# Normalised x of batches 2 to 7 is transposed by 32 x 32 turns on VectorE and sixteen transfers per batch, instead of on TensorE

## The reference, cut to what matters

```python
xn = layernorm(x)                        # per row of 128
q, k = rope(xn @ Wq.T), rope(xn @ Wk.T)  # 16 heads of 8; rope's angle is the batch's
v = xn @ Wv.T
attn = softmax(q @ k.T / sqrt(8)) @ v    # per batch and head, 512 x 512
# experts: sigmoid router (32 experts in 8 groups of 4, best 4 groups, best 6 experts)
moe = sum_e combine[:, e] * relu(xn @ up[e].T) ** 2 @ down[e].T      # 32 experts, 64 wide
shared = relu(xn @ shared_up.T) ** 2 @ shared_down.T                 # 256 wide
out = x + attn + moe + shared
```

## Time and profile before

| what | us |
|---|---|
| three runs, median (lowest to highest) | 612.33 (611.86 to 616.31) |
| the profiled execution, its own time | 611.43 |
| its span, first to last instruction | 609.6 |
| TensorE busy in it | 603.1 |
| VectorE, ScalarE, GpSimd busy in it | 425.5, 407.9, 428.4 |

### The profile page before, as it was taken

One profiled execution on the slowest core, in us unless ns is written; L12 is line 12 of the kernel. 1 busy time (PEld: TensorE's weight loads), 2 busy tenths in 40 slices (PEclk: granted clock), 3 DMA queues, 4 the chain that ended last, 5 costly groups with the idle time before them and its releaser, 6 DMA issues.

```text
span 609.6 us, 20168 instructions
## 1 busy us (share of the span) xinstructions
PE 603.1 (99%) x8269; PEld 269.1 (44%) x8269; DVE 425.5 (70%) x1058; ACT 407.9 (67%) x803; POOL 428.4 (70%) x512
## 2 busy tenths in 40 slices
PE   9999999999999999999999999999999999999997
PEld 7432544444444444434444434454443444444343
DVE  7898965777767776677867778586766877666402
ACT  3578667766776666766667676676667666666664
POOL 5850478677896778867788678876776767667653
PEclk9999999999999999999999999999999999999999
DMA  5176743646446254652437454263544634343430
GB/s 149 32 218 200 165 115 88 216 105 158 111 94 206 59 151 111 205 145 70 122 80 243 106 154 104 68 209 85 140 112 145 191 80 113 75 106 71 106 72 18
DMA packets 52029, 76.19 MB, mean 125 GB/s; under 512 B 5985, under 2 KB 19169, under 8 KB 51937
## 3 DMA queue, kind: packets, MB, share of 16 engines
q1 hardware_dynamic: 51916, 74.90, 45.6%
q10 hardware_dynamic: 20, 0.00, 0.0%
HBM read 56.14 MB, written 18.35 MB: 122 GB/s over the span
## 4 chain that ended last, share of the span: by engine, by line
PE 95%; DVE 2%; DMA 1%; SPq 1%; ACT 0%; issue 0%; DVEq 0%
PE acc L1060 21%; PE pv L1227 20%; PE st L1060 15%; PE upb L1060 10%; PE st L1197 9%; PE sc L1186 6%; PE upb L1197 4%; PE st L1202 3%; PE upb L1202 2%; PE sc L1119 1%; PE st L1169 1%; DVE nmax L930 1%; SPq L361 1%; DMA stacks<-k_stack 1%; DMA k_stack<-qk_parts 1%; PE upb L1169 1%
## 5 line engine op out<-in xcount | busy, mean ns | idle before, releaser
L930 DVE TENSOR_REDUCE nmax<-sc 128x1 f32<-128x512 f32 x512 | 328.5, 686 | 142.7 <-PE sc L1186 131.7
L700 ACT ACTIVATE probs<-st 128x512 f32<-128x512 f32 x359 | 202.8, 595 | 29.1 <-PE st L1202 19.3
L558 POOL TENSOR_TENSOR gated<-gate_at,relu 128x512 f32<-128x512 f32 x111 | 142.0, 1280 | 98.3 <-ACT relu L705 92.0
L562 POOL TENSOR_TENSOR g<-gated,relu 128x512 f32<-128x512 f32 x111 | 142.2, 1281 | 16.2 <-POOL gated L558 0.4
L1202 PE MATMUL st<-stacks 32*128 32x512 f32 x359 | 148.6, 577 | 0.0
L1227 PE MATMUL pv<-probs,v_aug 128*32 128x512 f32 x1024 | 136.4, 605 | 0.1
L1060 PE MATMUL acc<-dn,g 128*32 128x128 f32 x3512 | 134.8, 274 | 0.0
L1186 PE MATMUL sc<-stacks 32*128 32x512 f32 x512 | 132.6, 493 | 0.9 <-DMA stacks<-k_stack 0.4
L1060 PEld LDWEIGHTS acc<-dn,g 128*32 128x32 f32 x3512 | 112.2, 114 | 22.3 <-issue 22.1
L700 ACT ACTIVATE probs<-upb 128x512 f32<-128x512 f32 x153 | 91.0, 595 | 21.0 <-PE st L1202 14.2
L1197 PE MATMUL st<-m_rows,ones 3*128 3x512 bf16 x359 | 99.6, 384 | 0.3 <-ACT sh L682 0.3
(11 more groups left out here) (186 smaller groups left out, 565.4 us busy)
## 6 DMA issues: line engine op xcount, KB each, us to landing
gate_at<-gate_rows SPq DMA_DIRECT2D x62, 512.0 KB, 6.6
stacks<-q_stack SPq DMA_DIRECT2D x30, 256.0 KB, 6.7
stacks<-k_stack SPq DMA_DIRECT2D x30, 256.0 KB, 6.8
q_stack<-qk_parts SPq DMA_DIRECT2D x28, 256.0 KB, 6.6
k_stack<-qk_parts SPq DMA_DIRECT2D x28, 256.0 KB, 5.7
x_res<-in_x SPq DMA_DIRECT2D x8, 256.0 KB, 7.8
out<-y SPq DMA_DIRECT2D x8, 256.0 KB, 7.3
m_rows<-m_parts SPq DMA_DIRECT2D x95, 4.0 KB
```

The source lines that it names most:

```text
L558: nc.gpsimd.tensor_tensor(gated[:, u % 2, :], gate_at[:, group % RING, u % GATES, :], relu[:, u % RELUS, :], ALU.mult).then_inc(gated_read ...
L562: nc.gpsimd.tensor_tensor(g[:, u % 2, :], gated[:, u % 2, :], relu[:, u % RELUS, :], ALU.mult).then_inc(g_ready, 1)
L700: nc.scalar.activation(probs[:, u % 2, h, :], ring_b("st", u * QUAD + h)[:], ACT.Exp).then_inc(probs_ready, 1)
L930: nc.vector.tensor_reduce(out=nmax[:, s % 2, at:at + 1], in_=sc_b[tile % SC_BANKS][:], op=ALU.max, axis=AXX, negate=True).then_inc(s_read, 1)
```

## The change

For batches 2 to 7 the transposes on TensorE, their use of the ring and the copy on ScalarE go. In the same unit VectorE turns the 128 x 512 normalised rows in blocks of 32 x 32 (`turn_x`), into a new tile `x_blk`, laid out so that the piece of 32 columns c of x stands together. After it, SP issues sixteen transfers (`move_x`): for each c and each block a of 32 partitions, the blocks go from partitions 32 a on to partitions 32 c on of `xnT`, 32 partitions x 4 tiles x 32 numbers of 4 bytes, 16 KB. SP does this at the head of step j = 0 of batches 0 to 5, ahead of `load_max` of the next step, and waits there for VectorE. TensorE's projections and `make_half` wait for all sixteen (`x_moved`). GpSimd waits, before it overwrites half of `xn`, for the turn instead of the transposes. VectorE waits, before it overwrites `x_blk`, for the moves of the batch before. A unit that held the transposes no longer counts as `whole`. The first two batches are transposed as before.

```diff
@@ ring_order
                 if b + 2 < B:
-                    if n == (X_UNIT if b else X2_UNIT):
-                        order += [("x", b + 2)]
@@ SP
+            def move_x(i):
+                sp.wait_ge(x_turned, i - 1)
+                rows = xnT[:, i * T:(i + 1) * T].rearrange("d (t a r) -> d t a r", t=TT, r=COL)
+                for c in range(P // COL):
+                    for a in range(P // COL):
+                        sp.dma_start(rows[c * COL:(c + 1) * COL, :, a, :], x_blk[a * COL:(a + 1) * COL, :, c, :]
+                                     ).then_inc(x_moved, 16)
...
             for s in range(STEPS):
                 b, j = s // NQ, s % NQ
+                if j == 0 and b + 2 < B:
+                    move_x(b + 2)
@@ GpSimd, normalise
                 if tiles[0] == 0:
-                    wait(pool, xnT_psum, i - 1)
+                    wait(pool, xnT_psum, min(i - 1, 2))
+                    wait(pool, x_turned, i - 3)
@@ ScalarE, side_out
                 if b + 2 < B:
-                    if n == (X_UNIT if b else X2_UNIT):
-                        turned_out(b + 2)
@@ VectorE
+            def turn_x(i):
+                dve.wait_ge(xn_ready, i)
+                wait(dve, x_moved, (i - 2) * X_MOVES * 16)
+                nc.vector.transpose(x_blk[:].rearrange("p t c r -> p (t c r)"), xn[:, i % 2, :, :].rearrange("p t d -> p (t d)")
+                                    ).then_inc(x_turned, 1)
...
                 if n == SUM_UNIT and b:
                     add_residual(b - 1)
+                if n == (X_UNIT if b else X2_UNIT) and b + 2 < B:
+                    turn_x(b + 2)
@@ TensorE
                 att = kt == ATT_KT and q and q % PAIR == 0
-                return att or (b + 2 < B and n == (X_UNIT if b else X2_UNIT)) or u == UNITS - 1
+                return att or u == UNITS - 1
...
             def project(i, w, at=slice(0, T)):
-                pe.wait_ge(xnT_ready, i + 1)
                 if i > 1:
+                    pe.wait_ge(x_moved, (i - 1) * X_MOVES * 16)
                     bank_free("qk", 2 * i + w)
+                else:
+                    pe.wait_ge(xnT_ready, i + 1)
...
                 made = V_HALVES * (i - 1) + k
+                if i > 1:
+                    pe.wait_ge(x_moved, (i - 1) * X_MOVES * 16)
                 bank_free("v", made)
...
                 if b + 2 < B:
-                    if n == (X_UNIT if b else X2_UNIT):
-                        transpose_x(b + 2)
```

More of the change, by code:

```diff
@@ L50 @@
 STORES = 8
+X_MOVES = 16
 LOADS = 2
@@ L133, in build @@
         x_first = gate_at[:].rearrange("p r g t -> p (r g t)").rearrange("p (n d) -> p n d", d=D)
-        x_next = sb("x_next", [P, TT, D]); xn = sb("xn", [P, 2, TT, D])
+        x_next = sb("x_next", [P, TT, D]); x_blk = sb("x_blk", [P, TT, P // COL, COL]); xn = sb("xn", [P, 2, TT, D])
         stats = sb("stats", [P, TT * FIRST_X, 6]); mv = sb("mv", [P, NT, 2])
@@ L191, in build @@
         xn_first = sem("xn_first"); xn_ready = sem("xn_ready"); xnT_psum = sem("xnT_psum"); xnT_ready = sem("xnT_ready")
-        xnT_half = sem("xnT_half")
+        xnT_half = sem("xnT_half"); x_turned = sem("x_turned"); x_moved = sem("x_moved")
         logit_psum = sem("logit_psum"); exp_ready = sem("exp_ready"); sig_ready = sem("sig_ready")
@@ L623, in turned_out @@
                 act.wait_ge(xnT_psum, i + 1)
-                src = up_b if i == 0 else pv_b if i == 1 else ring_b("x", i)
+                src = (up_b, pv_b)[i]
                 nc.scalar.activation(xnT[:, i * T:i * T + n], src[:, 0:n], ACT.Copy).then_inc(xnT_ready, 1)
@@ L1082, in bank_free @@
                     pe.wait_ge(gT_ready, i + 1)
-                elif kind == "x":
-                    pe.wait_ge(xnT_ready, i + 1)
                 elif kind == "qk":
@@ L1090, in transpose_x @@
                     pe.wait_ge(xn_ready, i)
-                if i > 1:
-                    bank_free("x", i)
                 for t in range(TT):
@@ L1095, in transpose_x @@
                         pe.wait_ge(xn_first, t + 1)
-                    to = st_b[0] if i == 0 and t * P >= XN_HALF else up_b if i == 0 else pv_b if i == 1 else ring_b("x", i)
+                    to = st_b[0] if i == 0 and t * P >= XN_HALF else (up_b, pv_b)[i]
                     last = nc.tensor.transpose(to[:, t * P:(t + 1) * P], xn[:, i % 2, t, :], ident[:])
```

## The result

The changed kernel takes 648.48 us (median of six runs, 646.39 to 650.30) beside 612.55 for the kernel before in the same comparison: ratio 1.0572, 95% interval 1.0532 to 1.0613. The forecast was 630, in 615 to 645. Slower was right; the loss is 36 us instead of 18.

A forecast was written before the change was run, and what follows sets the result against it. TensorE was taken to bound the kernel. Waits behind SP's sixteen issues cost 7.7 us in batch 0 and 10.5 in batches 1 to 5, 18.2 in all with the gains inside: 630 us, range 615 to 645.

The forecast's parts named there:

- What bounds the kernel, and what goes: TensorE, busy 603.1 of 609.6 us, bounds the kernel; dropping the transposes saves 0.44 us per batch if nothing waits.
- The price of one issue: On SP, one move's issue takes 0.60 us, like the maxima's rows; sixteen take 9.6 us.
- the pieces are little for the DMA engines: A batch's 2048 short pieces, spread over 9.6 us of issuing, do not set the end unless at their upper estimate.
- Batch 0: Moves on SP delay the maxima's rows for step 1, so TensorE's unit 4 begins 7.7 us late.
- The wait of 7 to 8 us: Sign to look for: TensorE waits this long in front of unit 4 of batch 0, ended by the maxima's rows.
- Batches 1 to 5: TensorE waits for the moves before the values' products in unit n = 3: +2.1 us per batch, 10.5 for five.
- No second wait: Maxima's rows behind the moves land at 197.6 in batch 2, before TensorE reaches unit n = 4 at about 198.6.
- rival (b): TensorE's clock falls in the new waits: once, in batch 0, 633 us; at all six, 16.8 us, 647.
- the clock falling at most waits: Outcome in which TensorE's clock falls at most of the new waits, 640 to 650 us; chance 0.10.
- (a): Cheap issues on SP, 0.36 us each: net +1.7 us, 614, not slower; chance of 613 to 618 us 0.18.
- (c): Slow issues on SP, 0.92 us each: batch 0 +12.8 us, five batches about +7 each, 660; chance 0.08.
- (d): Faster by over 1%, needing 6 us, only from a stall that vanishes with the freed PSUM bank; chance 0.02.

The follow-up runs named there:

- experiment 4: Kernel before, transposes kept, plus the turn and the sixteen moves per batch into a tile that nobody reads: 646.51 us, ratio 1.0563.
- experiment 6: Changed kernel with later readers of the moved data (values at n = 6, q at n = 5, pieces of q's split a unit later): 656.50 us, ratio 1.0701.
- experiment 5: Kernel of experiment 1 with eight of the sixteen transfers per batch, half of xnT of batches 3 to 7 left as zeros: 610.25 us, ratio 0.9963.
- experiment 7: Changed kernel with experiment 1's batch 2, late readers, and the block of moves halved around the maxima's rows: 634.23 us, ratio 1.0371.
- experiment 1: Changed kernel with batch 2 transposed on TensorE again, so that batch 0 has no block of moves: 637.72 us, ratio 1.0409.
- experiment 8: As experiment 7, but SP issues ten moves, the maxima's rows, the gates' loads, then six moves; GpSimd's split keeps its batch 0 units: 628.74 us, ratio 1.0258.
- experiment 3: Changed kernel with 11 matmuls of a blank tile on TensorE ahead of the wait for the moves in batches 1 to 5: 640.17 us, ratio 1.0461.

## Why the prediction was wrong

*What bounds the kernel, and what goes*: right. A wait of TensorE counts in full, and the saving was 0.46 us in its unit (0.44 forecast), 0.33 net per batch.

*The price of one issue*: right in kind, and nearly in value. The 0.60 us was three of the maxima's rows with their gaps; the median move takes 0.602 without its gap of 0.04, so 0.645. The block is 10.45 to 11.8 us long instead of 9.6: 0.64 of it are the gaps, and the rest one or two issues in each block that take up to 1.4 us. That the pieces are little for the DMA engines holds too: their share was 0.14 in the wait of batch 1.

*Batch 0*: right to 0.4 us at unit 4, 7.26 against 7.7, at the place and by the transfer named. The closeness is partly luck: the block began at 40.48 instead of 41.58, since the residual's issue ahead of it took 2.56 us instead of 3.69, and that made up for a block 0.85 us longer. The wait of 7 to 8 us that was named as a sign measured 2.47, mainly because TensorE ran at the low clock ahead of it. What was missing is the 2.4 us that the batch loses afterwards at the low clock, and 0.6 in unit 8. That no reserve gives it back held.

*Batches 1 to 5*: right mechanism, undersized. The forecast of 2.1 us net per batch was idle time of 2.5 less the saving; the waits measured 2.71, 3.56, 3.26, 3.91 and 3.42. The longer block, 11.1 us on average, explains it; in batch 2 TensorE went on 1.29 us after the block ended (1.3 forecast). Five batches: 15.2 us net against 10.5.

*"No second wait"* was right as a reading and too weak as a thought: experiment 4 shows that the rows behind the moves arrive late by themselves, hidden by the first wait. Whoever removed the first wait (experiment 6) got the second.

*The step that failed* is the clock. I had it as rival (b), priced it at 2.8 us a wait and 16.8 us for all six, 647 us in all, and then gave "the clock falling at most waits" a chance of 0.10 and put no clock into the sum. It was low behind all six: 10.9 us in five batches (2.2 each) and 2.4 in batch 0, 13.3 us. The error of 18.2 us is 13.3 of clock, 4.7 of longer waits, 0.6 of unit 8 and -0.4 of batch 0 up to unit 4. That the rival's total of 647 came so close to 648.48 is partly luck as well: its clock is 3.5 us too dear, and its waits are 4.7 too short. My reason against it, that no wait of this trace is long enough to show it, spoke for neither side: the kernel before has no idle stretch of TensorE as long as 1 us after its start-up, so it could not show what a wait of 2.5 us does. The start-up rows were the only evidence, and their slow pace spoke for the fall, though the clock that the profile grants there is 1.00 (1.04 to 7.36 us), so they show a pace and not a low clock. Rivals (a) and (c) are out by the issue price, (d) by the unit times.

*Open*: the low clock lasts 3.4 to 6.8 us in batches 1 to 5, but 10 to 20 in batch 0 (about 20 in the changed kernel, 10 in experiment 6); in the changed kernel it had fallen there at 39.5 us, behind an idle stretch of 1.01 us and ahead of the long wait; in experiments 4 and 6 it fell only in that wait. What decides this was not settled. It matters little for the sum: up to unit 4 SP's queue sets the time, and the other five runs of the changed kernel take 646.39 to 650.30 us with mean clocks of 0.968 to 0.976 instead of 0.963.

## What to carry to other kernels

Before moving a step to DMA, count its issues and multiply by the nearest measured issue in the queue that will carry them; compare that block, not the bytes, with the slack of everything queued behind it, and leave room inside the block for what is urgent. A wait of TensorE that the trace of before does not contain is priced at its length plus the slow work behind it, unless a row shows that the clock survives it. When a wait is moved, look for the next one it was hiding: queue order, a helper engine's list and a ring of buffers each took their turn here.

## What the runs showed of the hardware

Sixteen transfers of 16 KB between partitions, in 128 pieces of 128 bytes, take SP 10.5 to 11.8 us, 0.60 us for the median issue and 0.04 from one to the next; half as many take 5.2 to 5.7 (experiment 5). Over the block of batch 2 the DMA engines are busy for 0.47 of the time (199.5 to 210.5 us), while the load of the stack ahead of it still runs, and towards its end, from 206 to 210 us, for 0.17: the issuing, not the moving, is the price. The Trainium skill, "Perfetto Trace Analysis" (What "DMA-bound" means), lists the issuing sequencer as a bound of its own; SP's solid block here is such a case.

TensorE's granted clock fell to 0.50, 1.2 GHz, in or behind nearly every idle stretch of 1.96 to 8.46 us in these runs (one of 2.35 us, in batch 1 of experiment 4, had no fall) and cost about 2.2 us each time in batches 1 to 5 of the changed kernel. It fell behind one of 1.73 us (experiment 7, batch 0) and after one of 1.01 us (changed kernel, batch 0) too, but not behind one of 1.58 us (experiment 1) nor those of 0.73 to 1.54 us of experiment 8's profiled run. So these runs show no length of idle time that decides it. Twenty-two instructions on a blank tile in the wait, 2.72 us, kept it at 2.4 GHz, in all five batches of experiment 3.

VectorE's turn of 128 x 512 numbers of 4 bytes in blocks of 32 x 32 takes 0.70 us, as long as a maximum over as many (0.685 on average).
